# Layer 1 of a two-layer gated attention and MoE kernel: 32 output projections ahead of the routed tiles

## The reference

```python
s = attn @ Wo.T + bo
h = silu(x @ w_gate.T) * (x @ w_up.T)      # 176 wide, per expert
moe = sum_e h_e @ w_down_e.T * combine[:, e] + shared(x)
```

## Time and profile before

| what | value |
|---|---|
| median of 3 runs | 1857.05 us (1850.56 to 1860.44) |
| the profiled execution | 1867.35 us |
| its span, first to last instruction | 1865.6 us |
| mean granted TensorE clock | 0.936 |
| PE busy | 1618.1 us (87%) |
| DVE busy | 1373.3 us (74%) |
| ACT busy | 1032.9 us (55%) |
| POOL busy | 672.2 us (36%) |

### The profile page before, as it was taken

One profiled execution on the slowest core, in us unless ns is written; L12 is line 12 of the kernel. 1 busy time (PEld: TensorE's weight loads), 2 busy tenths in 40 slices (PEclk: granted clock), 3 DMA queues, 4 the chain that ended last, 5 costly groups with the idle time before them and its releaser, 6 DMA issues. The chain is left out here.

```text
span 1865.6 us, 34560 instructions
## 1 busy us (share of the span) xinstructions
PE 1618.1 (87%) x9650; PEld 1253.5 (67%) x9650; DVE 1373.3 (74%) x3710; ACT 1032.9 (55%) x2457; POOL 672.2 (36%) x842
## 2 busy tenths in 40 slices
PE   6897787679983776999999999997889999988997
PEld 5786676569982554554555555544789999967775
DVE  6778999256667887999888888832666666657777
ACT  2555465246664761466576767664556666643443
POOL 2545588410007633121236767620000000056662
PEclk9898899889995996899999999998999999999998
DMA  9322456654444887242354546414964444355552
GB/s 345 120 69 68 96 134 183 173 162 131 132 123 138 275 298 210 58 110 62 70 125 134 175 135 176 129 40 133 274 186 133 131 132 132 119 158 170 164 167 77
DMA packets 291879, 272.72 MB, mean 146 GB/s; under 512 B 138153, under 2 KB 260714, under 8 KB 289644
## 3 DMA queue, kind: packets, MB, share of 16 engines
q1 hardware_dynamic: 267960, 215.41, 39.9%
q0 software_dynamic: 18432, 50.36, 8.9%
q10 hardware_dynamic: 5332, 4.96, 0.8%
HBM read 136.84 MB, written 133.69 MB: 145 GB/s over the span
## 5 line engine op out<-in xcount | busy, mean ns | idle before, releaser
L1880 ACT ACTIVATE ca_PT<-ca_psS 128x512 f32<-128x512 f32 (+3 forms) x768 | 336.4, 494 | 206.0 <-PE ca_psS L1917 201.0
L1421 POOL DMA_INDIRECT g_y<-ys_scratch,pos x128 | 125.0, 977 | 434.7 <-POOLq L73 363.7
L1796 DVE CUSTOM_DVE_ANT_0 ca_masked_row<-ca_psM,mask_row 128x384 f32<-128x384 f32 (+3 forms) x512 | 224.2, 485 | 44.8 <-PE ca_psM L1900 42.7
L1917 PE MATMUL ca_psS<-ca_QS,ca_KS 128*128 128x512 f32 (+1 forms) x480 | 175.4, 369 | 1.4 <-ACT ca_PT L1880 1.4
L1800 DVE TENSOR_REDUCE ca_part<-ca_psM 128x1 f32<-128x512 f32 x256 | 163.6, 684 | 17.0 <-PE ca_psM L1900 15.6
L1929 PE MATMUL ca_psO<-ca_PT,ca_VA 128*17 128x512 f32 (+3 forms) x1536 | 163.1, 497 | 6.0 <-ACT ca_OT L1872 6.0
L790 PE MATMUL fa_psO<-fa_weighed,ident 128*128 128x256 f32 x512 | 132.0, 416 | 38.1 <-DVE fa_weighed L585 38.1
L1900 PE MATMUL ca_psM<-ca_KS,ca_QS 126*128 126x512 f32 (+2 forms) x480 | 159.5, 380 | 5.5 <-DVE ca_part L1796 4.3
L1917 PEld LDWEIGHTS ca_psS<-ca_QS,ca_KS 128*128 128x128 f32 x480 | 90.8, 190 | 87.4 <-ACT ca_PT L1880 58.5
L790 PEld LDWEIGHTS fa_psO<-fa_weighed,ident 128*128 128x128 f32 x512 | 104.9, 210 | 59.8 <-DVE fa_weighed L585 44.4
L391 POOL DMA_INDIRECT xs_scratch<-x_sb,pos x128 | 124.6, 973 | 55.9 <-ACT ca_PT L1880 34.2
(11 more groups left out here) (271 smaller groups left out, 4656.1 us busy)
## 6 DMA issues: line engine op xcount, KB each, us to landing
xs_scratch<-fa_blank SPq DMA_DIRECT2D x32, 640.0 KB, 4.9
x_sb<-xs_scratch SPq DMA_DIRECT2D x143, 128.0 KB, 2.1
ys_scratch<-x_sb SPq DMA_DIRECT2D x143, 128.0 KB, 1.7
xs_scratch<-fa_blank SPq DMA_DIRECT2D x32, 384.0 KB, 6.7
spare<-qk_scratch SPq DMA_DIRECT2D x24, 512.0 KB, 7.4
ca_QS<-qk_scratch SPq DMA_DIRECT2D x20, 512.0 KB, 6.2
ca_KS<-qk_scratch SPq DMA_DIRECT2D x20, 512.0 KB, 7.8
x_sb<-in_ffn SPq DMA_DIRECT2D x16, 608.0 KB, 4.1
```

The costliest lines, as they stand in the source:

```text
L1421: pool.indirect_dma_start(y[:, t % R, k, :], None, y_dram, bass.IndirectOffsetOnAxis(pos[:, t, k:k + 1], 0)).then_inc(got[t % R], 16)
L1796: ins = dve.tensor_tensor_reduce(masked_row[:, (n * NU + u) % BANKS, h * w:(h + 1) * w], bank[:, h * w:(h + 1) * w], mask_row[:, CHUNK - w ...
L1880: act.activation(PT[:, s % PTS, h, off:CHUNK], psS[(GH * s + h) % BANKS][:, off:CHUNK], ACT.Exp)\
L1917: pe.matmul(psS[tile % BANKS][:, off:CHUNK], KS[slot][:, h, kt * P:(kt + 1) * P], QS[slot][:, h, c * CHUNK + off:(c + 1) * CHUNK], start=T ...
```

## The change

Layer 1's call passes `lag=E1 + 1`, 17 instead of the default 2 (layer 0's call has `lag=E0 + 1` in both kernels):

```diff
--- before.py
+++ after.py
@@ -2089,7 +2089,7 @@
                 for w in range(early.WB):
                     sp.dma_start(early.w_raw[:, w, :], a["shared1"][w]).then_inc(early.w_in[w], 16)
             project_beside_experts(nc, "f1", o_tile, 1.0, None, s1_dram, a["ffn1"], E1, SLOTS1, te[1], w_hi, w_lo, xs_dram[1], ys_dram[1],
-                                   ident, early, load_last=load_shared)
+                                   ident, early, load_last=load_shared, lag=E1 + 1)
         shared_and_gate(nc, "g1", a["shared1"], xt_dram, ys_dram[1], pos[1], wts[1], got[1], sig, x1_dram, s1_dram, out_v, early)
```

## The result

| | before | changed |
|---|---|---|
| median of 4 runs | 1858.74 us | 1885.82 us (1873.38 to 1890.03) |
| profiled execution, its span | 1867.35, 1865.6 us | 1890.03, 1888.2 us |
| mean granted clock | 0.936 | 0.931 |
| PE busy | 1618.1 us | 1620.0 us |

The ratio is 1.0134, 95% interval 1.0102 to 1.0167: 25 us slower, 19 to 31. The forecast was +25 us, 1882 us in a range of 1864 to 1893. PE's work is the same within 2 us; what is new is waiting, in the one phase that the change touches. From the start of its first copy of an attention tile to the start of the last copy of a routed tile's result it took 1280.65 to 1634.13, 353.5 us, before and 1281.11 to 1656.73, 375.6 us, now: +22.1 in these two executions.

The account below looks back on a forecast made before the run. The ramp was taken as paced by SP's weight load waiting for an older split, the rest as TensorE-bound; 10.8 us of longer ramp plus 14.1 of tiles gave +25 on 1857, 1882 us, range 1864 to 1893.

Parts of the forecast that it names:

- ramp: Layer 1's phase from first attention-tile transpose to last high half: 80.1 us before, 90.9 after, 10.8 us longer.
- Steps 0 to 7: Projections alone: 21.8 us for 16 tiles plus 1.7 for half clock, 23.5; first high half at 26.3 us.
- store round: Steps 0 to 7: layer 1's stores through four buffers pace projections, 5.45 us for four tiles with a 2.5 us landing.
- Steps 8 to 15: Projections and splits: three rounds of 10.0 us plus 1.5 for half clock, 34.5 us; expert 6 at 60.8 us.
- half-clock rival: TensorE stays at half clock: rounds of 12.2 us, 8 for two steps in 17 to 23; +32, 1889 us; chance 0.20.
- Steps 16 to 23: Splits with the first seven tiles: four rounds of 6.8 us, expert 15 some 2.9 later, at 90.9 us.
- Tiles: Seven routed tiles no longer ride in the ramp's gaps, at 2.02 us of TensorE time each: 14.1 us.
- The loads of the next phase: Issued in step 39 instead of 23, stalling the tile loads behind them as much as before: no change.
- Throughput: Rival: DMA throughput bound the ramp, so fewer bytes shorten its steps; +8, 1865 us; chance 0.13.
- 10.0 us round: Ramp before: split, weight load, attention tiles queued behind it, projections, next split; 10.0 us for two steps, 5.0 a step.
- closed-round line: Expectation for e2: 3.4 us a step, the 16 steps from 80 to 54 us, time down 20 us or more.

Follow-up runs that it names:

- e4: The changed kernel with routed tiles 9 steps behind instead of 17, splits still from step 8 on: ratio 1.0048 to the kernel before.
- e6: The changed kernel with splits from step 0 on as before the change, routed tiles still 17 steps behind: ratio 1.0214 to the kernel before.
- e1: The changed kernel with SP's two attention-tile loads ahead of the weight load in each step of layer 1's phase: ratio 1.0070 to the kernel before.
- e2: The kernel before with SP's attention-tile loads ahead of the weight load in layer 1's phase: ratio 0.9951 to the kernel before.
- e11: The kernel before with attention tiles loaded first, the next phase's loads spread and splits last in a step: ratio 0.9909, 1841.66 us.
- e5: The changed kernel with 11 filler matmuls, results unused, ahead of steps 10, 12 and 14: ratio 1.0118 to the kernel before.

## Why the prediction was right

**The sum.** +25 us was forecast, +25 (19 to 31) measured; in the two profiled phases +22.1, which is 10.5 of ramp (10.8 forecast) and 14.0 of tiles (14.1 forecast), less 1.8 for the shorter distance between tiles in the profiled execution of the changed kernel and 0.5 for a shorter stall. So the mechanism and its two main terms hold; that the times agree to the microsecond is chance within ±6 us. By its steps, counted as there from the first transpose (1280.41 now):

- *Steps 0 to 7*: the first high half was put at 26.3 us and came at 22.9. The step that was too large is mainly the store round. It was charged to all 16 tiles. The trace has 1.08 us a copy from 1285.65 to 1289.99 and 1.31 from there to 1303.04: 5.2 us for four where I had 5.45, but on ten tiles only, since the first stores are not waited for. The landing, taken as 2.5 us, was:

```profile
DMA to landing us min/median/max: 1.7/2.5/3.5
```

- *Steps 8 to 15*: three rounds of 11.5 forecast, 12.4, 12.4 and 12.2 measured, 37.0 for 34.5 us. The term that was too small is the clock's: from the first transpose to the high half it took 4.9 us (1310.79 to 1315.69), 4.9 and 4.4 instead of 2.76, so half clock cost 2.0 a round on average where 1.5 was charged. The rest is the landing behind the weight load, 4.3, 4.4 and 4.7 us from issue to transpose for 4.2 before, charged with nothing. The rounds are thus the size of the half-clock rival's 12.2 (its own terms, 10.0 and twice 1.05, make 12.1); its other claim, 8 us for two steps from 16 on, did not hold, they took 6.9.
- *Steps 16 to 23*: four rounds of 6.8 forecast, 6.9 measured, and the last expert 3.1 us later for 2.9. Together the last high half was forecast at 90.9 us and stood at 90.6. That it comes so near is luck: 3.4 us too much in the first stretch and 3.1 too little in the other two cancelled.
- *Tiles*: seven riders fewer, at 2 us each. The last column of the table and e4, e6 show this term by itself, over 0 to 15 riders.
- *The loads of the next phase*, at nothing: ACT waited 4.10 us for the tile behind them in step 39's stall, for 4.71 in step 23's, and the whole stall was 6.9 us for 7.4 (about 7 was forecast):

```profile
1413.07 0.38 ACT L1036 ACTIVATE f_x_hi<-f_psT 128x256 fp32r<-128x256 f32 x1 [4.10 <-PE f_psT L982]
```

**The rivals.** Throughput was the rival on the other side. e1 decides against it for the changed kernel: another order of the same loads took 12 us out. The forecast's argument for it, 95% busy engines, was no evidence: e2 and e11 have the same share at 285 and at 302 GB/s. Whether the 256-byte pieces of the attention tiles cost more than their bytes, no run here tests. The Trainium skill's "TensorE: Matmul & The Clock Gate", section "HAM oscillation", was weighed as a rule that speaks against the change; the trace agrees, each round's first matmuls are at half clock (1.91 us). e5 puts the worth of it at about 3 us of the ramp.

**Where the reasoning was too simple.** "No instruction of a routed tile is in it" is true of the 10.0 us round, but a second round with the tile's x_lo in it lay only 0.2 us a step below. The sum did not need it, since steps without routed tiles don't have it; anyone who had forecast e2 from the first round alone, as its closed-round line does, would have been 10 us off.

## What to carry to other kernels

Where a phase has a stretch with slack ahead of a stretch that is bound by one engine, write its time as the length of the first plus the bound engine's time for whatever did not ride in it; moving work out of the slack costs its full time, even if the slack then looks tidier. Read the bound engine's time per tile in each execution anew before two phases are compared to a microsecond: here it alone made 1.8 us. Before trusting a wait's name, ask what stands in front of the awaited transfer in its issuing queue: here one exchange of two loads was worth as much as half the change. And when a limit is removed and the gain is a fraction of what was due, halve the next suspect instead of believing it, even when the number fits.

## What was not expected of the hardware

- A DMA share of 1.01 was reached at 285 GB/s (e2) and at 302 GB/s (e11) with the same kinds of transfers; a share of 1 did not mark the end of throughput.
- A 256-column float32 matmul shows as two records of 0.216 us at full clock: 20 fillers are 40 records and took 8.64 us. Who reads records as matmuls prices them at half.
- The phase began between 1265.45 and 1282.66 us in executions whose code ahead of it is the same. Behind the phase they are alike, 230.8 to 232.5 us from its last result to the end. Most of their scatter arises ahead of the phase; what causes it was not tried.
- With PE full, the distance between routed tiles was either 2.006 us or 1.992 to 1.993 us in the thirteen profiled executions, whatever the kernel.
